# State space scan: ScalarE scales the turned u, TensorE turns it back, twelve states of sixteen

## The chip, the cores and the metric

The kernel runs on one core of one Trainium2 chip. The time is the device time of one execution in microseconds (us), as the median of several runs. Before the change it is 4166.02 us (three runs, 4165.89 to 4167.23).

## What is computed

The reference is a chain of four blocks over x of 8 sequences x 1024 tokens x 256 features. The change touches the first of them, a selective state space model with 16 states for each of 256 channels:

```
dt = softplus(x @ W_dt + b_dt);  A = -exp(A_log);  Bm = h @ W_B;  Cm = h @ W_C
decay = exp(dt[..., None] * A)                    # (T, B, D, N)
inp = (dt * x)[..., None] * Bm[:, :, None, :]     # (T, B, D, N), N = 16
s = decay * s + inp                               # over t, in order
y = einsum('bdn,bn->bd', s, c)                    # c = Cm at t
y = y + D_skip * x
```

Below, u = dt * x. For each state n, sequence b and half h of the channels (128 on the partitions), the input of the scan is u times the row B[n, :] over the 1024 tokens.

## The kernel before, in words

The program is a list of phases, one after the other: `ssm_inputs`, `ssm_scan`, `ssm_output`, then the delta, attention and expert phases. Only `ssm_scan` is touched. It goes through 8 batches (the sequences), each with 16 states n and 2 halves h, in this order; `own = n * H + h` (H = 2) numbers the 32 scans of a batch, `at` numbers them over all batches: 256 scans. Batches 1 to 6 run in a loop of three rounds with two batches each, the first and the last stand outside it.

For one scan:
- ScalarE makes the decay, exp(dt * A), 128 x 1024 elements (L606), into one of four buffers; it waits until the scan four before is done.
- The input, u times B's row, is put into PSUM, into `psI[h]`. There is one such tile for each half, so the input of scan k + 2 can only be made when scan k is done. For the states of `DIAG` (even n) TensorE does it: u was turned once for a batch, in chunks of 128 tokens (L632, copied by ScalarE to `uT`, L584), ScalarE fills `diag` with the identity times B's column of that chunk (L592, 8 instructions for a state, in two parts after each of the two exponentials of the state before, two buffers), and TensorE multiplies the turned u with it (L645, 8 chunks). For the states of `MIXED` (odd n) VectorE multiplies u by B's row, which a DMA has spread over the partitions (L703, right behind the scan before).
- VectorE scans (L724): `tensor_tensor_scan` over the 1024 tokens, decay and `psI[h]` in, one of four `state` buffers out.
- GpSimd multiplies the state by C's row (L575), into one of eight buffers `prod`.
- TensorE adds this to y in PSUM by a product with the identity (L656, two of 512 columns), three scans later (`LAG`). In its queue the step `own` holds the turn of the next u where it is due, then the input for scan `own + 1`, then the accumulation of scan `own - 3`.
- When the 16 states of a half are through, VectorE adds D_skip * x to y (L710, after scans 2 and 3 of the next batch), and the accumulation of the next batch's first state in that half waits for it.

Each engine has its own queue and works in order. They wait for one another by counting semaphores (`state_ready`, `inp_ready`, `dec_ready`, `prod_ready`, `y_added`, `uT_ready`, `diag_ready`). The turn of the next batch's u goes through `psI` too, at own = `TURN - 1` and `TURN`, where the states are mixed and TensorE doesn't need `psI`; `TURN` = `MIXED[3] * H` = 14. VectorE's L703 of that state waits until ScalarE has copied the turned u out (L701, L702). SyncE issues the loads; rows of B (512 KB, L520) are loaded for the mixed states alone.

Of the kernel before, what the change touches and what calls it, by code (L numbers as in the profile page):

```python
# [448 lines left out]
def ssm_scan(nc, A):  # L449
    CHUNKS = T // P  # L450
    ROWS = 4
    MIXED = tuple(range(1, S, 2))
# [3 lines left out]
    with ExitStack() as ctx:  # L456
# [6 lines left out]
        uT = [[m.sb(f"uT{k}{h}", [P, CHUNKS, P]) for h in two] for k in two]  # L463
        diag = [m.sb(f"diag{k}", [P, CHUNKS, P]) for k in two]
# [11 lines left out]
        diag_ready, dec_ready, inp_ready, state_ready = m.sem("diag"), m.sem("dec"), m.sem("inp"), m.sem("state")  # L476
# [4 lines left out]
        TURN = MIXED[3] * H  # L481
# [16 lines left out]
        with nc.Block() as block:  # L498
# [82 lines left out]
            def _(act):  # L581
                def turned(b, k, h):
                    act.wait_ge(u_turned, b * H + (h + 1))
                    act.activation(uT[k][h][:], psI[1 - h][:] if isinstance(b, int) and b == 0 else psI[h][:],  # L584
                                   ACT.Copy).then_inc(uT_ready, 1)

                def fill(b, n, part):

                    if part == 0 and (not isinstance(b, int) or b > 0 or DIAG.index(n) >= 2):
                        act.wait_ge(inp_ready, diag_count(b, n, 1) - 2 * H)  # L590
                    for c in range(4 * part, 4 * part + 4):
                        act.activation(diag[DIAG.index(n) % 2][:, c, :], ident[:], ACT.Copy,  # L592
                                       scale=b_col[:, bass.ds(b * CHUNKS + c, 1), n]).then_inc(diag_ready, 1)

                def batch(b, k, place):
                    for n in range(S):
                        for h in two:
# [9 lines left out]
                            if n in DIAG:  # L607
                                then = n + 1 if n + 1 in DIAG else n + 2
                                if then < S:
                                    fill(b, then, h)  # L610
                                elif place < 3:
                                    fill(b + 1, then - S, h)
# [9 lines left out]
                for h in two:  # L622
                    fill(0, 0, h)
                turned(0, 0, 1)
                act.wait_ge(a_made, 1)
# [3 lines left out]
            def _(pe):  # L629
# [5 lines left out]
                def scan_input(b, k, own, place):  # L635
# [3 lines left out]
                    pe.wait_ge(diag_ready, (b * ND + (order + 1)) * CHUNKS)  # L639
# [4 lines left out]
                    for c in range(CHUNKS):  # L644
                        last = pe.matmul(psI[h][:, c, :], uT[k][h][:, c, :], diag[order % 2][:, c, :], start=True, stop=True)  # L645
# [13 lines left out]
                def batch(b, k, place):  # L659
                    for own in range(PER):  # L660
# [9 lines left out]
                        elif H < own + 1 < PER and (own + 1) // H in DIAG:  # L670
# [2462 lines left out]
```

## Time and profile before

| | us |
|---|---|
| median of three runs | 4166.02 |
| profiled execution, its own time | 4168.11 |
| span of its instructions | 4166.5 |
| TensorE / VectorE / ScalarE / GpSimd busy | 3502 / 3254 / 2306 / 1370 |
| first scan starts, last starts | 272.2, 1070.8 |

The shares of busy time over the whole span mix eight phases with different limits. The scan is the stretch from some 250 to some 1080 us. One line of a view by line stands for all instructions of that line and shape: count, busy time (the union of their times), mean duration of one in ns, and the idle time of the engine just before them with what ended it. fp32 matmuls are recorded twice for each call, as they go through the array twice; a transpose is recorded once.

### The profile page before, as it was taken

What the parts mean: (1) busy time and instruction counts of PE and PEld (TensorE: products, weight loads), DVE (VectorE), ACT (ScalarE), POOL (GpSimd) and SP (SyncE); (2) the same over time, 40 slices, a digit from 0 to 9 for tenths busy, and PEclk for the clock granted to TensorE, in tenths of its full rate; (3) what the DMA queues carried; (4) which work ended last, traced back from release to release, by engine and by line L of the source; (5) the groups of instructions that cost most, each with busy time, mean ns of one, the idle gap of its engine ahead of it and who ended that gap; (6) DMA issues with size and microseconds to landing.
All of it is one profiled execution on the core that took longest, in us unless ns stands there. A gap on an engine that the chain in (4) does not pass through costs nothing. (4 is left out here: it accounts for less than half of the span.)

```text
span 4166.5 us, 65564 instructions
## 1 busy us (share of the span) xinstructions
PE 3502.2 (84%) x20079; PEld 2104.2 (51%) x20080; DVE 3253.8 (78%) x4239; ACT 2306.2 (55%) x4128; POOL 1369.6 (33%) x905
## 2 busy tenths in 40 slices
PE   8969888888657979989799999999999965379950
PEld 3445555555346868878233333333333324279950
DVE  8959999999786645657889898989899823368868
ACT  6755555555594533311288888888888851033323
POOL 4448888889302445410000000000000004645530
PEclk9989999999888989999599999999999985589975
DMA  6665444454677943377123232322222114222348
GB/s 218 248 207 175 164 163 162 162 172 137 206 253 189 253 119 106 91 195 221 40 52 74 52 73 52 71 55 64 61 59 66 30 42 133 89 77 90 92 159 293
DMA packets 536067, 538.10 MB, mean 129 GB/s; under 512 B 85296, under 2 KB 441776, under 8 KB 535648
## 3 DMA queue, kind: packets, MB, share of 16 engines
q1 hardware_dynamic: 521856, 497.23, 40.8%
q0 software_dynamic: 13952, 37.74, 2.6%
q8 instruction: 123, 2.02, 0.2%
q14 instruction: 136, 1.11, 0.1%
HBM read 317.93 MB, written 215.71 MB: 128 GB/s over the span
## 5 line engine op out<-in xcount | busy, mean ns | idle before, releaser
L2321 DVE TENSOR_REDUCE at_top<-at_psM 128x1 f32<-128x1024 f32 x1024 | 1206.1, 1220 | 136.5 <-PE at_psM L2172 135.4
L2281 ACT ACTIVATE at_probs<-at_psS 128x512 f32<-128x512 f32 x2048 | 1060.9, 603 | 250.8 <-PE at_psS L2198 250.8
L2198 PE MATMUL at_psS<-at_q,at_k 64*128 64x512 f32 x2048 | 795.3, 468 | 8.3 <-ACT at_probs L2281 8.3
L575 POOL TENSOR_TENSOR sc_prod<-sc_state,sc_c_row 128x1024 f32<-128x1024 f32 x256 | 709.1, 2789 | 117.2 <-DVE sc_state L724 109.0
L2172 PE MATMUL at_psM<-at_k,at_q 62*128 62x512 f32 x2048 | 689.7, 451 | 36.5 <-DMA at_vraw<-scratch_vf 21.9
L724 DVE TENSOR_TENSOR_SCAN sc_state<-sc_dec,sc_psI 128x1024 f32<-128x1024 f32 x256 | 578.4, 2280 | 53.3 <-PE sc_psI L645 29.5
L2172 PEld LDWEIGHTS at_psM<-at_k,at_q 62*128 62x128 f32 x2048 | 313.1, 190 | 601.8 <-DVE at_top L2321 519.8
L2211 PE MATMUL at_psV<-at_probs,at_v 128*32 128x512 f32 x4096 | 546.3, 605 | 0.0
L656 PE MATMUL sc_psY<-sc_prod,sc_ident 128*128 128x512 f32 x1024 | 467.4, 597 | 3.5 <-DVE sc_y L710 2.2
L606 ACT ACTIVATE sc_dec<-sc_dt,sc_a_exp 128x1024 f32<-128x1024 f32 x256 | 293.6, 1148 | 311.1 <-DVE sc_state L724 308.3
L2198 PEld LDWEIGHTS at_psS<-at_q,at_k 64*128 64x128 f32 x2048 | 337.6, 184 | 195.5 <-ACT at_probs L2281 190.6
L2139 POOL COPY at_v<-at_vraw 128x256 f32<-128x256 f32 x32 | 12.9, 403 | 1253.1 <-DMA at_vraw<-scratch_vf 1169.4
L645 PE MATMUL sc_psI<-sc_diag,sc_uT 128*128 128x128 f32 x2048 | 266.9, 285 | 91.8 <-DVE sc_state L724 86.9
L645 PEld LDWEIGHTS sc_psI<-sc_diag,sc_uT 128*128 128x128 f32 x2048 | 245.6, 196 | 184.2 <-DVE sc_state L724 136.8
L656 PEld LDWEIGHTS sc_psY<-sc_prod,sc_ident 128*128 128x128 f32 x1024 | 185.6, 193 | 185.2 <-issue 173.1
L2765 POOL DMA_INDIRECT scratch_ys<-ex_y,ex_slot x156 | 172.0, 1103 | 185.1 <-DVE ex_y L2898 138.9
L2352 PEld LDWEIGHTS ex_psY<-ek_w,ex_hid 128*128 128x128 f32 x1872 | 223.8, 188 | 3.9 <-issue 1.0
L2352 PE MATMUL ex_psY<-ek_w,ex_hid 128*128 x1872 | 224.9, 279 | 0.6 <-DVE ex_hid L2891 0.6
L703 DVE TENSOR_TENSOR sc_psI<-sc_u,sc_b_row 128x1024 f32<-128x1024 f32 x128 | 171.1, 1337 | 8.7 <-ACT sc_uT L584 8.7
L2491 POOL DMA_INDIRECT scratch_xs<-er_rows,ek_spot x128 | 129.5, 1012 | 115.9 <-DVE ek_spot L2652 72.6
L592 ACT ACTIVATE sc_diag<-sc_ident,sc_b_col 128x128 f32<-128x128 f32 x512 | 161.7, 387 | 6.3 <-PE sc_psI L645 6.3
L2785 ACT ACTIVATE ex_xT<-ex_psT 128x512 fp32r<-128x512 f32 x39 | 23.4, 600 | 253.4 <-PE ex_psT L2815 253.4
(393 smaller groups left out, 4941.4 us busy)
## 6 DMA issues: line engine op xcount, KB each, us to landing
sc_c_row<-scratch_bc SPq DMA_DIRECT2D x128, 512.0 KB, 4.3
scratch_xs<-at_zeros SPq DMA_DIRECT2D x140, 264.0 KB, 4.7
sc_b_row<-scratch_bc SPq DMA_DIRECT2D x64, 512.0 KB, 5.1
ec_y<-scratch_ys SPq DMA_DIRECT2D x32, 512.0 KB, 6.4
ex_x<-scratch_xs SPq DMA_DIRECT2D x39, 264.0 KB, 3.1
si_x<-in_x SPq DMA_DIRECT2D x16, 512.0 KB, 4.4
scratch_xn<-si_xn SPq DMA_DIRECT2D x16, 512.0 KB, 5.1
scratch_x_t<-si_xT SPq DMA_DIRECT2D x16, 512.0 KB, 5.7
```

The costliest lines, as they stand in the source:

```text
L575: pool.tensor_tensor(prod[:, (n * H + h) % 8, :], state[slot][:], c_row[n % ROWS][:], ALU.mult).then_inc(prod_ready, 1)
L606: act.activation(dec[slot][:], dt[k][h][:], ACT.Exp, scale=a_exp[:, h, n:n + 1]).then_inc(dec_ready, 1)
L645: last = pe.matmul(psI[h][:, c, :], uT[k][h][:, c, :], diag[order % 2][:, c, :], start=True, stop=True)
L656: last = pe.matmul(psY[h][:, cols], ident[:], prod[:, own % 8, cols], start=(n == 0), stop=(n == S - 1))
L724: dve.tensor_tensor_scan(state[slot][:], dec[slot][:], psI[h][:].rearrange("p c t -> p (c t)"), 0.0, ALU.mult, ALU.add).then_inc(state_rea ...
L2172: ins = pe.matmul(psM[t % 2][:, half * TILE:(half + 1) * TILE], rows_of(q4[j], h, 0, MAXROW)[:, c * P:(c + 1) * P], rows_of(k4[j], h, 0, M ...
L2198: pe.matmul(psS[v % 3][:], rows_of(k4[j], h, 0, GROUP)[:, c * P:(c + 1) * P], rows_of(q4[j], h, 0, GROUP)[:, half * TILE:(half + 1) * TILE ...
L2211: last = pe.matmul(psV[32 * h:32 * h + 32, :], v4[j][:, c, h, :], probs[:, slot(j, at_slot[4 * g + n]), :], start=(c == 0), stop=(c == KC ...
L2281: act.activation(probs[:, slot(j, v), :], psS[v % 3][:], ACT.Exp).then_inc(act_done, 1)
L2321: dve.tensor_reduce(top[j % 2][:, h, c:c + 1], psM[t % 2][:], AX.X, ALU.max, negate=True).then_inc(maxed, 1)
L2352: last = pe.matmul(out, a, b, start=start and n == 0, stop=stop and n == len(parts) - 1)
L2765: pool.indirect_dma_start(out=A["ys"], out_offset=bass.IndirectOffsetOnAxis(ap=slot[par][:, s:s + 1], axis=0), in_=y[par][:, s, :], in_off ...
```

## The change

Four states stay with VectorE (2, 6, 10, 14); the other twelve get their input from TensorE, in another way. ScalarE no longer scales the identity by B's column. It scales the turned u itself, both halves in one instruction: `scaled` is 128 tokens x 8 chunks x (2 x 128 channels), and each of the 8 instructions for a state is 256 elements wide instead of 128. TensorE then turns each chunk back (a transpose with the identity) into `psI[h]`. So `uT` becomes one tile for both halves, the first fill of a batch waits until both halves of u are turned, and `TURN` becomes `MIXED[2] * H` = 20.

```diff
-    MIXED = tuple(range(1, S, 2))
+    MIXED = (2, 6, 10, 14)
...
-        uT = [[m.sb(f"uT{k}{h}", [P, CHUNKS, P]) for h in two] for k in two]
-        diag = [m.sb(f"diag{k}", [P, CHUNKS, P]) for k in two]
+        uT = [m.sb(f"uT{k}", [P, CHUNKS, H, P]) for k in two]
+        scaled = [m.sb(f"scaled{k}", [P, CHUNKS, H, P]) for k in two]
...
-        TURN = MIXED[3] * H
+        TURN = MIXED[2] * H
...
-                    act.activation(uT[k][h][:], psI[1 - h][:] if isinstance(b, int) and b == 0 else psI[h][:],
+                    act.activation(uT[k][:, :, h, :], psI[1 - h][:] if isinstance(b, int) and b == 0 else psI[h][:],
...
-                def fill(b, n, part):
+                def fill(b, k, n, part):
 
                     if part == 0 and (not isinstance(b, int) or b > 0 or DIAG.index(n) >= 2):
                         act.wait_ge(inp_ready, diag_count(b, n, 1) - 2 * H)
+                    if DIAG.index(n) == 0:
+                        act.wait_ge(uT_ready, b * H + H)
                     for c in range(4 * part, 4 * part + 4):
-                        act.activation(diag[DIAG.index(n) % 2][:, c, :], ident[:], ACT.Copy,
-                                       scale=b_col[:, bass.ds(b * CHUNKS + c, 1), n]).then_inc(diag_ready, 1)
+                        act.activation(scaled[DIAG.index(n) % 2][:, c, :, :], uT[k][:, c, :, :], ACT.Copy,
+                                       scale=b_col[:, bass.ds(b * CHUNKS + c, 1), n]).then_inc(scaled_ready, 1)
...
                             if n in DIAG:
-                                then = n + 1 if n + 1 in DIAG else n + 2
-                                if then < S:
-                                    fill(b, then, h)
+                                order = DIAG.index(n) + 1
+                                if order < ND:
+                                    fill(b, k, DIAG[order], h)
                                 elif place < 3:
-                                    fill(b + 1, then - S, h)
+                                    fill(b + 1, 1 - k, DIAG[0], h)
...
-                for h in two:
-                    fill(0, 0, h)
                 turned(0, 0, 1)
+                for part in two:
+                    fill(0, 0, 0, part)
...
-                    pe.wait_ge(diag_ready, (b * ND + (order + 1)) * CHUNKS)
+                    pe.wait_ge(scaled_ready, (b * ND + (order + 1)) * CHUNKS)
...
-                        last = pe.matmul(psI[h][:, c, :], uT[k][h][:, c, :], diag[order % 2][:, c, :], start=True, stop=True)
+                        last = pe.transpose(psI[h][:, c, :], scaled[order % 2][:, c, h, :], ident[:])
...
-                        elif H < own + 1 < PER and (own + 1) // H in DIAG:
+                        elif H <= own + 1 < PER and (own + 1) // H in DIAG:
```

## Rows read from the trace of the kernel before

**Rows 1.** The page: busy time by engine, and one group of its section 5.

```profile
PE 3502.2 (84%) x20079; PEld 2104.2 (51%) x20080; DVE 3253.8 (78%) x4239; ACT 2306.2 (55%) x4128; POOL 1369.6 (33%) x905
...
L2281 ACT ACTIVATE at_probs<-at_psS 128x512 f32<-128x512 f32 x2048 | 1060.9, 603 | 250.8 <-PE at_psS L2198 250.8
```

**Rows 2.** By stretch: busy PE, PEld, DVE, ACT, POOL; clock, DMA share, GB/s.

```profile
474.00:576.00 102.00, 88.76 (x398) 54.02 (x397) 93.44 (x51) 56.63 (x98) 88.76 (x33) 0.98 0.50 172
```

**Rows 3.** By tile, sc_psI: count, duration ns min/median/max, first and last start us.

```profile
L724 DVE TENSOR_TENSOR_SCAN sc_state<-sc_dec,sc_psI x256: 2258/2286/2289, 272.2 to 1070.8; 128x1024 f32<-128x1024 f32 x128
```

**Rows 4.** By line, 272.2 to 1073.1 us: count, busy, mean, idle, releasers.

```profile
L575 POOL TENSOR_TENSOR sc_prod<-sc_state,sc_c_row 128x1024 f32<-128x1024 f32 x255 | 706.8, 2790 | 117.0 <-DVE sc_state L724 108.8 <-issue 7.9
L724 DVE TENSOR_TENSOR_SCAN sc_state<-sc_dec,sc_psI 128x1024 f32<-128x1024 f32 x256 | 578.4, 2280 | 53.3 <-PE sc_psI L645 29.5 <-DVE sc_psI L703 9.0 <-ACT sc_dec L606 8.3
...
L703 DVE TENSOR_TENSOR sc_psI<-sc_u,sc_b_row 128x1024 f32<-128x1024 f32 x128 | 171.1, 1337 | 8.7 <-ACT sc_uT L584 8.7
...
L710 DVE SCALAR_TENSOR_TENSOR sc_y<-sc_x,sc_skip,sc_psY 128x1024 f32<-128x1024 f32 x14 | 17.7, 1265 | 0.0
```

**Rows 5.** By tile, sc_prod: the same columns as rows 3.

```profile
L575 POOL TENSOR_TENSOR sc_prod<-sc_state,sc_c_row x256: 2347/2370/3356, 274.6 to 1073.1; 128x1024 f32<-128x1024 f32 x128
```

**Rows 6.** VectorE timeline, steady step: start us, length us, count, [idle before].

```profile
541.64 1.21 DVE L703 TENSOR_TENSOR sc_psI<-sc_u,sc_b_row 128x1024 f32<-128x1024 f32 x1
543.04 6.87 DVE L724 TENSOR_TENSOR_SCAN sc_state<-sc_dec,sc_psI 128x1024 f32<-128x1024 f32 x3 [0.19 <-ACT sc_dec L606]
549.83 1.35 DVE L703 TENSOR_TENSOR sc_psI<-sc_u,sc_b_row 128x1024 f32<-128x1024 f32 x1
...
553.57 1.21 DVE L703 TENSOR_TENSOR sc_psI<-sc_u,sc_b_row 128x1024 f32<-128x1024 f32 x1
```

**Rows 7.** Timeline, VectorE after the loop's jump back at some 571 us.

```profile
575.11 2.29 DVE L724 TENSOR_TENSOR_SCAN sc_state<-sc_dec,sc_psI 128x1024 f32<-128x1024 f32 x1 [3.75 <-PE sc_psI L645]
...
586.62 4.46 DVE L724 TENSOR_TENSOR_SCAN sc_state<-sc_dec,sc_psI 128x1024 f32<-128x1024 f32 x2
...
602.44 2.29 DVE L724 TENSOR_TENSOR_SCAN sc_state<-sc_dec,sc_psI 128x1024 f32<-128x1024 f32 x1 [1.68 <-PE sc_psI L645]
```

**Rows 8.** Timeline around a turn of u: scan input, accumulation, transposes, VectorE's L703.

```profile
507.28 2.05 PE L645 MATMUL sc_psI<-sc_diag,sc_uT 128*128 128x128 f32 x16
...
509.17 1.88 PE L656 MATMUL sc_psY<-sc_prod,sc_ident 128*128 128x512 f32 x4
...
510.46 0.14 PEld L632 LDWEIGHTS sc_psI<-sc_ident,sc_u 128*128 128x128 f32 x1 [0.24 <-issue]
510.88 1.04 PE L632 MATMUL sc_psI<-sc_ident,sc_u 128*128 128x128 f32 x8
...
511.76 1.88 PE L656 MATMUL sc_psY<-sc_prod,sc_ident 128*128 128x512 f32 x4
...
513.01 2.37 DVE L703 TENSOR_TENSOR sc_psI<-sc_u,sc_b_row 128x1024 f32<-128x1024 f32 x1 [1.21 <-ACT sc_uT L584]
```

**Rows 9.** Timeline of ScalarE: fills of the diagonal, exponentials back to back.

```profile
265.35 2.43 ACT L592 ACTIVATE sc_diag<-sc_ident,sc_b_col 128x128 f32<-128x128 f32 x8
...
273.00 3.22 ACT L606 ACTIVATE sc_dec<-sc_dt,sc_a_exp 128x1024 f32<-128x1024 f32 x3
```

**Rows 10.** Timeline of TensorE: transposes while the granted clock is 0.50.

```profile
262.42 3.67 PE L632 MATMUL sc_psI<-sc_ident,sc_u 128*128 128x128 f32 x16
```

**Rows 11.** Busy time by stretch at a batch's start: columns as in rows 2.

```profile
592.50:595.90 3.40, 1.15 (x8) 0.87 (x8) 3.21 (x3) 1.84 (x5) 2.96 (x2) 1.00 1.01 387
595.90:599.30 3.40, 3.40 (x13) 2.62 (x12) 3.21 (x3) 0.95 (x2) 3.05 (x2) 0.50 1.01 400
```

**Rows 12.** Delta stage by stretch: all, then L1591's transposes alone (PE, PEld, clock).

```profile
1722.30:1725.70 3.40, 2.09 (x17) 1.88 (x18) 1.82 (x8) 1.19 (x2) 2.45 (x2) 1.00 0.06 16
...
1722.30:1725.70 3.40, 1.28 (x8) 0.84 (x8) 1.00 0.06 16
```

More of the change, by code:

```diff
@@ L475, in ssm_scan @@
         b_turned, b_ready, u_turned, uT_ready = m.sem("b_turned"), m.sem("b_ready"), m.sem("u_turned"), m.sem("uT_ready")
-        diag_ready, dec_ready, inp_ready, state_ready = m.sem("diag"), m.sem("dec"), m.sem("inp"), m.sem("state")
+        scaled_ready, dec_ready, inp_ready, state_ready = m.sem("scaled"), m.sem("dec"), m.sem("inp"), m.sem("state")
         prod_ready, y_added, y_ready = m.sem("prod"), m.sem("y_added"), m.sem("y_ready")
```

## The prediction, made before the change was timed

> **What bounds the kernel now.** I read the page first [rows 1], and then only the state space scan, the one stage that the diff touches. It is bounded by four engines at once. One stretch of it shows VectorE busy 93 of 102 us, TensorE 89, GpSimd 89 and ScalarE 57, with the granted clock at 0.98 [rows 2], so what counts is how they hand work on. The scans (L724) start at 272.2 and the last ends at 1070.8 + 2.3 = 1073.1 us [rows 3]: 801 us of the run, and everything outside it stays as it is. In it VectorE has 256 scans, 128 products u·B (L703) and 14 outputs (L710): 578.4 + 171.1 + 17.7 = 767 us [rows 4], so VectorE sets the end. GpSimd's 707 us are inflated: a product costs 2.37 us in the median but 2.79 in the mean and up to 3.36 [rows 4, 5]. Taken one by one, those that overlap an L703 are the long ones.
>
> The steady step is read from VectorE's timeline [rows 6]. Two states (four scans: two mixed, two diagonal) take 553.57 - 541.64 = 11.93 us. The L703 at 541.64 holds the next scan back until 543.04, 1.40 us; the one at 549.83 holds the diagonal-to-mixed passage, and 549.83 to 553.57 is that L703 with its scan, 3.74 us. With 2.21 us for the scan this L703 costs 1.53, and the three scans between take 6.79, 2.26 each. 64 such steps make 764 us. The remaining 37 us are the 14 outputs (17.7), the seven turns of u (idle 8.7 in all), and some 11 us after idle ends at TensorE, among them 3.75 where the loop jumps back [rows 4, 7].
>
> **Part 1: VectorE.** Eight states were mixed, now four: 64 of the 128 L703 go. At (1.40 + 1.53)/2 = 1.46 each this is 94 us off VectorE. This is the most that the change can give.
>
> **Part 2: GpSimd.** It gets no new work and loses half of the overlaps. Before: 256 x 2.36 = 604 us if undisturbed, and 707 in fact, 103 more or 0.8 for each L703. Half of this goes, which leaves about 655 us. Per eight scans (the new pattern: one mixed state, three others): 8 x 2.36 + 2 x 0.8 = 20.5 us.
>
> **Part 3: TensorE.** The diagonal matmul goes through twice per chunk (16 records for 8 chunks); 507.28 to 509.17 is its hold on the engine, 1.89 us per scan input. The new transposes have the form of L632, which is one record per chunk. In the stream at full clock it holds the engine from 510.88 to 511.76, 0.88 us for eight [rows 8]. An accumulation into y (four records) holds it 510.88 - 509.17 = 1.71 us. Per eight scans TensorE had 4 x 1.89 + 8 x 1.71 = 21.2 us and gets 6 x 0.88 + 8 x 1.71 = 19.0. So the sum falls, but not where it hurts. In three neighbouring unmixed states each scan brings 0.88 + 1.71 = 2.6 us to TensorE and 2.26 to VectorE. I walked such a run of six scans: psI is single per half, so the input for scan k+2 can start only when scan k is over. Let the last mixed scan end at 0. The first input starts at 0.05 and takes 1.04 [rows 8] and 0.05 to be seen: ready at 1.14. The following start at 2.65, 5.25, 7.85, 10.45, each ready 1.1 later, at 11.55 the last. Scans want to start at 2.3, 4.5, 6.8, 9.1, 11.3. The first three inputs are in time, the fourth just, the fifth is 0.2 late. The run ends at 13.9 instead of 13.6 us. In the mixed state that follows, TensorE has 2 x 1.71 us of work in 7.4 us and catches up.
>
> So eight scans take 13.9 + 1.40 + 2.21 + 1.53 + 2.21 = 21.25 us, and 32 of them 680, against 764 before: **84 us less** (the 94 of part 1, less 10 that the runs give back).
>
> **Part 4: ScalarE.** L592 was 128 elements wide, 8 per state; it becomes 256 wide, 8 per state, and there are 12 states instead of 8. Its pace is 2.43/8 = 0.30 us, that of the exponentials (3.22 - 1.14)/2 = 1.04 us for 1024 elements [rows 9], which is 0.83 ns an element, so 0.30 + 0.11 = 0.41 us for 256. Bounds: 0.30 (width costs nothing), and 0.52, the pace of 512 wide (1060.9/2048) [rows 1]; I take 0.41. Per eight scans: 6 x (1.04 + 4 x 0.41) + 2 x 1.04 = 18.2 us, under 21.25. It is also early enough: the fill of a scaled buffer waits for the inputs of the state two before. In the run above the third state's fill can start at 1.14, and ends with the exponential between at 1.14 + 4 x 0.41 + 1.04 + 4 x 0.41 = 5.5; its input wants to start at 7.85. Nothing on the path, at 0.52 neither (6.3).
>
> **Part 5: what is moved.** The turn of the next u moves from state 7 to state 10, behind a full run. There TensorE is 1.7 us late instead of caught up, ScalarE then copies for 1.0 us, and VectorE's L703 waits for that: I get 1.35 us where the trace has 1.21 [rows 8], and over seven turns 1 us. The second copy of a turn now stands behind four wider fills on ScalarE (1.64 instead of 1.2 us) and is still in time. At the very start both copies and one fill of 8 x 0.41 precede the first input; but eight transposes replace sixteen passes at low clock (16 took 3.67 us there [rows 10]), so the first scan starts within 0.3 us of 272.2. Half of the 64 loads of B rows leave SyncE's queue; no transfer is waited for now, and no bound moves. The loop's jump back (3.75 us of idle, twice) stays.
>
> **Part 6: the clock.** At the batch's start, mixed state 2 stands behind two outputs on VectorE. TensorE cannot start y's accumulation for half 1 before the second output, and has no scan input to do meanwhile. I get 2.6 us of idle, then another 0.7 and 1.1. The trace shows what follows such a hole: TensorE busy 1.15 of 3.4 us, then clock 0.50 for the next 3.4 [rows 11], and then VectorE waits 1.68 us [rows 7]. This happened at two of seven batches before; I expect it at five or six, some at twice the length: 9 us more (bounds: 0, and 24 for seven twice 1.7).
>
> **Sum:** -84 + 1 + 9 + 1 (start, tail) = **-73 us**. The profiled execution (4168.1 us, 2.1 above the median of the runs) becomes 4095, the median **4093**.
>
> **A rule against it.** In the delta stage TensorE did transposes for 1.28 of 2.09 busy us in a stretch of 3.4, and the granted clock stayed at 1.00 [rows 12]. The Trainium skill (TensorE: Matmul & The Clock Gate, Part 4: PE-mode transpose) says the opposite: the full clock doesn't engage for transposes, they don't count as busy the same way. By that rule rival A below would be the case; by the row only the holes of part 6 count.
>
> **Rivals.**
> A. *The low clock wins (slower).* If transposes don't hold the clock up, TensorE falls to 1.2 GHz in the runs. Transposes took 3.67/16 = 0.23 us there [rows 10] against 0.11, so all of its work doubles: 38 us per eight scans, 1216 for the stage and the rest of 46: 460 us slower, about 4628. It decides from a share f of low clock at which 19.0 (1 + f) passes the 801/32 = 25.0 us of before: f = 0.32. For it: transposes are done in three of four states. The rule of the Trainium skill named above speaks for it as well. Against it: rows 12, and that accumulations stay 13.7 of every 19.0 us. Chance 0.06.
> B. *The hand-off is slower than my walk.* If a transpose batch that waited for its semaphore can't be prefetched, it holds TensorE for 0.42 us more (its first weights are loaded at 510.46, its first pass is at 510.88 [rows 8]), the pace in a run is 3.0, and its last input is ready at 13.2: 1.6 us more per run, 51 in all, so a gain of 22 us: 4144. Or ScalarE's wide copies double with their width, to 0.6: 6 x (1.04 + 2.4) + 2.08 = 22.7 us per eight scans, 47 us more: 4140. Both have milder forms; I put 4111 to 4156 here. Chance 0.22.
> C. *Full gain.* Two scans with early input run at (4.46 - 2.29) = 2.17 us apart [rows 7], less than 2.26. If TensorE keeps up and the clock stays, the whole 94 us and a little more come: 4062 to 4076. Chance 0.10.
> D. *The change doesn't do what it says:* the transposes of the scaled copies go through twice like matmuls. TensorE then has 6 x 1.89 + 13.7 = 25.0 us per eight scans, as much as the stage has now, and the runs are bound by 3.6 us a scan: 20.4 a run (the first input has 1.2 us of slack) and 7.35 for the mixed state, 27.8 x 32 = 889: 125 more than 764, 4293. Rows 8 speak against it. Chance 0.02.
> Something that just cancels the gain: 0.02. The forecast itself, 4076 to 4111: 0.58.
>
> **How the numbers follow.** The time is that of the forecast. From 4062 to 4135 lie C, the forecast and over half of B, about 0.82. A measurement of this kernel tells about 0.2% from no change, 8 us: faster is forecast, B and C, 0.90; A and D are slower, 0.08; 0.02 the same.
>
> **What the profile after would show.** 64 L703; scan inputs as 1536 single records, 8 in 0.9 us; ScalarE's fills at about 0.41 us pace and its busy time near 600 us in the stage; GpSimd's products 2.5 to 2.6 us in the mean; eight scans in 21.3 us; VectorE's idle before L724 put down to the transposes, small in the first half of a run and growing in its second; low clock after batch starts alone. I am wrong if VectorE waits in every scan of a run (B), if the clock is low inside runs (A), or if the fills set when transposes start.

## The result, and the profile after

The kernel after takes 4067.23 us (median of four runs, 4065.67 to 4072.39), beside 4165.95 for the kernel before on the same chip (4164.12 to 4167.23). The ratio is 0.977, with a 95% interval of 0.9757 to 0.9784: **99 us faster**, where 73 were forecast. It is inside the range of 4062 to 4135, but below the band of 4076 to 4111 that stood for the forecast's own mechanism, and inside the band of rival C. So two questions are open: which mechanism it was, and where some 25 us more come from. The profiled execution after has a time of its own of 4072.39, a span of 4070.8, so the profiled pair differs by 95.7. The page's busy time by engine, beside rows 1:

```profile
PE 3424.0 (84%) x19567; PEld 2028.8 (50%) x19568; DVE 3169.5 (78%) x4175; ACT 2440.9 (60%) x4384; POOL 1304.4 (32%) x905
```

VectorE has lost 84 us of work, GpSimd 65 without losing an instruction, and ScalarE has gained 135.

By line, from the first scan to the last, to be read against rows 4 (count, busy us, mean ns, idle before with its releasers). VectorE's product is now L705, the scan L726, the output L712, ScalarE's fill L594, GpSimd's product still L575:

```profile
L575 POOL TENSOR_TENSOR sc_prod<-sc_state,sc_c_row 128x1024 f32<-128x1024 f32 x255 | 646.4, 2564 | 84.4 <-DVE sc_state L726 73.5 <-PE sc_psY L658 5.8 <-issue 5.0
L726 DVE TENSOR_TENSOR_SCAN sc_state<-sc_dec,sc_psI 128x1024 f32<-128x1024 f32 x256 | 574.2, 2276 | 43.5 <-PE sc_psI L647 32.9 <-DVE sc_psI L705 6.9 <-POOL sc_prod L575 1.5
...
L594 ACT ACTIVATE sc_scaled<-sc_uT,sc_b_col 128x256 f32<-128x256 f32 x758 | 321.1, 494 | 95.3 <-PE sc_psI L647 95.3
...
L705 DVE TENSOR_TENSOR sc_psI<-sc_u,sc_b_row 128x1024 f32<-128x1024 f32 x64 | 86.1, 1346 | 8.7 <-ACT sc_uT L584 8.7
```

By tile, `sc_psI`, beside rows 3 (count, duration ns min/median/max, first and last start):

```profile
L647 PE MATMUL sc_psI<-sc_ident,sc_scaled x1536: 272/273/448, 271.1 to 976.4; 128*128 128x128 f32 x192
L726 DVE TENSOR_TENSOR_SCAN sc_state<-sc_dec,sc_psI x256: 2260/2286/2289, 273.0 to 977.6; 128x1024 f32<-128x1024 f32 x128
```

The change does what it says: 64 L705 instead of 128, and 1536 single records of transposes (12 states x 2 halves x 8 chunks x 8 batches), so rival D is out. From the first scan's start to the last's it is 704.5 us, where rows 3 give 798.6: **94.0 us of the 95.7 are in this stage**. Below, "the stage" is always this stretch, since it can be compared between chips. The waits of L726 for TensorE are 32.9 us where they were 29.5 [rows 4].

VectorE's timeline shows the steady pattern of eight scans (start us, length us, count, [idle before]):

```profile
570.50 1.21 DVE L705 TENSOR_TENSOR sc_psI<-sc_u,sc_b_row 128x1024 f32<-128x1024 f32 x1
571.90 2.29 DVE L726 TENSOR_TENSOR_SCAN sc_state<-sc_dec,sc_psI 128x1024 f32<-128x1024 f32 x1 [0.19 <-DVE sc_psI L705]
574.11 1.21 DVE L705 TENSOR_TENSOR sc_psI<-sc_u,sc_b_row 128x1024 f32<-128x1024 f32 x1
575.50 11.10 DVE L726 TENSOR_TENSOR_SCAN sc_state<-sc_dec,sc_psI 128x1024 f32<-128x1024 f32 x5 [0.19 <-DVE sc_psI L705]
586.91 2.29 DVE L726 TENSOR_TENSOR_SCAN sc_state<-sc_dec,sc_psI 128x1024 f32<-128x1024 f32 x1 [0.30 <-PE sc_psI L647]
589.50 2.29 DVE L726 TENSOR_TENSOR_SCAN sc_state<-sc_dec,sc_psI 128x1024 f32<-128x1024 f32 x1 [0.31 <-PE sc_psI L647]
593.00 2.33 DVE L705 TENSOR_TENSOR sc_psI<-sc_u,sc_b_row 128x1024 f32<-128x1024 f32 x1 [1.21 <-ACT sc_uT L584]
```

One scan of the pair in the mixed state stands at 571.90, the other at 575.50, 3.6 apart. The scans behind it need no wait until, at the end of the run, two wait 0.30 for TensorE, and they stand 589.50 - 586.91 = 2.59 apart. That is the 0.88 + 1.71 of the prediction. The eight steps of this group are 3.60, 3.60, 2.20, 2.18, 2.18, 2.25, 2.59, 2.59: **21.19 us, where 21.25 were forecast**. The same stretch of the other batches of the loop takes 21.2 to 21.3. Against 23.86 before (twice 11.93), over 32 such groups, this is 83 to 85 us less.

The other 10 us show in the lengths of batches (start of the first scan to that of the next batch). Before, the seven are 97.3, 99.8, 99.8, 104.7, 99.8, 104.5 and 99.8; after, 86.1, 89.2, 89.3, 89.4, 89.3, 89.1 and 89.1. **The two long batches are gone**: the fourth and the sixth, behind which the loop jumps back. That is 4.9 + 4.7 = 9.6 us. The sum of 93 to 95 stands against 94.0 measured. Two things lie in these 9.6, as the steps between scans show. The first step behind the jump is 3.5 and 3.3 us longer than in the other batches, 6.8 together. Some 30 us on, the scan at 602.44 that waits 1.68 for TensorE [rows 7] stands behind a stretch at clock 0.50 [rows 11]; there, and at the same place of the sixth batch, the steps are 1.4 longer, 2.8 together. The other batches of before have neither. The jump itself is visible in TensorE's queue, in the time of the branch at the loop's end (L486). First before, then after; count, duration ns min/median/max, first and last start; the 82 and 83 are the last round, where nothing is jumped:

```profile
L486 PEldq COMPARE_BRANCH  x3: 82/5062/5113, 566.1 to 974.9; - x3
```
```profile
L486 PEldq COMPARE_BRANCH  x3: 83/215/221, 535.5 to 892.5; - x3
```

Behind the jump of after, where a batch starts at 537.5, there is no 3.75 us hole as in rows 7:

```profile
530.78 11.20 DVE L726 TENSOR_TENSOR_SCAN sc_state<-sc_dec,sc_psI 128x1024 f32<-128x1024 f32 x5 [0.19 <-DVE sc_psI L705]
542.59 2.29 DVE L726 TENSOR_TENSOR_SCAN sc_state<-sc_dec,sc_psI 128x1024 f32<-128x1024 f32 x1 [0.61 <-POOL sc_prod L575]
```

The batch's beginning shows what became of the low clock:

```profile
550.47 2.28 DVE L726 TENSOR_TENSOR_SCAN sc_state<-sc_dec,sc_psI 128x1024 f32<-128x1024 f32 x1
552.67 1.20 DVE L705 TENSOR_TENSOR sc_psI<-sc_u,sc_b_row 128x1024 f32<-128x1024 f32 x1
554.06 6.64 DVE L726 TENSOR_TENSOR_SCAN sc_state<-sc_dec,sc_psI 128x1024 f32<-128x1024 f32 x3 [0.19 <-ACT sc_dec L608]
```

By stretch (busy PE, PEld, DVE, ACT, POOL; clock, DMA share, GB/s), the first beside rows 2, the others beside rows 11:

```profile
474.00:576.00 102.00, 92.33 (x381) 52.30 (x380) 95.70 (x49) 86.26 (x151) 93.11 (x38) 0.98 0.51 180
548.40:551.80 3.40, 1.20 (x3) 0.68 (x4) 3.40 (x3) 2.94 (x6) 3.18 (x1) 0.99 0.00 0
551.80:555.20 3.40, 3.40 (x11) 2.22 (x10) 3.21 (x3) 1.15 (x1) 2.29 (x1) 0.50 0.46 165
```

The clock falls behind TensorE's hole as it did before (busy 1.20 of 3.4 us, then 0.50, the level of 1.2 GHz). It does so at three of the seven batches, at 551.8, 640.5 and 729.3, each time for 3.4 us. But the three scans from 554.06 stand 2.2 apart without a wait: low clock and mixed state coincide, and there TensorE has time to spare.

### The profile page after: what moved, and what is told of

It reads as the page before. It is cut to its first block and busy times, and to the rows that moved or that the text cites. A ratio compares the mean times of both kernels' runs of the same rounds, so it can differ in the third digit from the quotient of the medians.

```text
span 4070.8 us, 64939 instructions
## 1 busy us (share of the span) xinstructions
PE 3424.0 (84%) x19567; PEld 2028.8 (50%) x19568; DVE 3169.5 (78%) x4175; ACT 2440.9 (60%) x4384; POOL 1304.4 (32%) x905
## 3 DMA queue, kind: packets, MB, share of 16 engines
q8 instruction: 103, 1.69, 0.2%
## 5 line engine op out<-in xcount | busy, mean ns | idle before, releaser
L575 POOL TENSOR_TENSOR sc_prod<-sc_state,sc_c_row 128x1024 f32<-128x1024 f32 x256 | 648.7, 2564 | 84.4 <-DVE sc_state L726 73.5
L726 DVE TENSOR_TENSOR_SCAN sc_state<-sc_dec,sc_psI 128x1024 f32<-128x1024 f32 x256 | 574.2, 2276 | 43.5 <-PE sc_psI L647 32.9
L658 PE MATMUL sc_psY<-sc_prod,sc_ident 128*128 128x512 f32 x1024 | 479.2, 598 | 15.6 <-DVE sc_y L712 15.6
L594 ACT ACTIVATE sc_scaled<-sc_uT,sc_b_col 128x256 f32<-128x256 f32 x768 | 325.2, 494 | 95.4 <-PE sc_psI L647 95.3
L608 ACT ACTIVATE sc_dec<-sc_dt,sc_a_exp 128x1024 f32<-128x1024 f32 x256 | 285.2, 1135 | 7.7 <-DVE sc_state L726 7.7
L647 PEld LDWEIGHTS sc_psI<-sc_ident,sc_scaled 128*128 128x128 f32 x1536 | 178.7, 143 | 179.2 <-DVE sc_state L726 82.6
L647 PE MATMUL sc_psI<-sc_ident,sc_scaled 128*128 128x128 f32 x1536 | 205.9, 278 | 60.5 <-DVE sc_state L726 53.6
L2213 PEld LDWEIGHTS at_psV<-at_probs,at_v 128*32 128x32 f32 x4096 | 80.6, 108 | 128.1 <-ACT at_probs L2283 85.6
```

What stands on the lines that cost most here:

```text
L575: pool.tensor_tensor(prod[:, (n * H + h) % 8, :], state[slot][:], c_row[n % ROWS][:], ALU.mult).then_inc(prod_ready, 1)
L594: act.activation(scaled[DIAG.index(n) % 2][:, c, :, :], uT[k][:, c, :, :], ACT.Copy, scale=b_col[:, bass.ds(b * CHUNKS + c, 1), n]).then_i ...
L608: act.activation(dec[slot][:], dt[k][h][:], ACT.Exp, scale=a_exp[:, h, n:n + 1]).then_inc(dec_ready, 1)
L647: last = pe.transpose(psI[h][:, c, :], scaled[order % 2][:, c, h, :], ident[:])
L658: last = pe.matmul(psY[h][:, cols], ident[:], prod[:, own % 8, cols], start=(n == 0), stop=(n == S - 1))
L726: dve.tensor_tensor_scan(state[slot][:], dec[slot][:], psI[h][:].rearrange("p c t -> p (c t)"), 0.0, ALU.mult, ALU.add).then_inc(state_rea ...
```

## The experiments

The stage of each, in us, and its difference from that of its base (before 798.6, after 704.5); expectations are on record as quoted. Ratios are to the kernel before on the same chip. The kernels that leave work out say so in their expectation.

| kernel | made from | ratio | stage | against its base |
|---|---|---|---|---|
| e1_odd_transposed | before, new method alone | 0.9972 | 787.7 | -10.9 |
| e2_diag_four | before, four mixed states alone | 1.0123 | 851.1 | +52.5 |
| e9_pe_half | after, half of TensorE's additions | 0.9757 | 699.7 | -4.8 |
| e10_pool_half | after, half of GpSimd's products | 0.9755 | 696.0 | -8.5 |
| e11_both_half | after, both halved | 0.9701 | 676.6 | -27.9 |
| e4_fill_split | after, twice the fills | 0.9872 | 746.6 | +42.1 |
| e3_quarters | after, longer loop on TensorE | 0.9791 | 709.1 | +4.6 |
| e6_before_unrolled | before, no loop | 0.9963 | 783.0 | -15.6 |
| e7_after_unrolled | after, no loop | 0.9755 | 697.7 | -6.8 |
| e8_early | after, mixed states one earlier | 0.979 | 708.6 | +4.1 |
| e5_two_mixed | after, two mixed states | 0.9738 | 686.3 | -18.2 |
| e12_changed_again | after, unchanged | 0.9765 | 705.6 | +1.1 |

The last row says how far two profiles of one kernel are apart: 1 us in the stage. The 95% intervals of the ratios reach 0.001 to 0.0045 to either side. By them e1, e2, e4, e6 and e11 differ from their bases; for the others the difference is read from the stage of one profile each.

**The halves of the change: method and number.** The new method with the eight mixed states of before:

```diff
-    MIXED = (2, 6, 10, 14)
+    MIXED = tuple(range(1, S, 2))
-        TURN = MIXED[2] * H
+        TURN = MIXED[3] * H
```

> The changed kernel with the eight odd states left to VectorE as before, so only the way of making the other inputs differs (scaled copies turned back). Theory (inputs that arrive earlier, and a TensorE loop that is short enough not to be fetched again): of four scans one that took 2.38 us before takes 2.2, 64 x 0.18 = 12 us, and the two long steps at the loop's jump (4.8 us each) go, 10 us: the scan stage takes 779 us instead of 799 to 801, the kernel is 20 to 22 us faster than before. Rival (only the number of products on VectorE counts): 0, within 3 us of before.

Ratio 0.9972 (0.9961 to 0.9983). The stage is 10.9 us shorter, and all of it but about one is the two long batches (its branch takes 0.22 us). The batches are 99.8 long as before, though the last scan of each run now comes after 2.18 instead of 2.38 us. The trace shows what eats this (both engines, same columns):

```profile
544.77 7.97 POOL L575 TENSOR_TENSOR sc_prod<-sc_state,sc_c_row 128x1024 f32<-128x1024 f32 x3 [0.36 <-DVE sc_state L726]
...
548.97 1.58 DVE L705 TENSOR_TENSOR sc_psI<-sc_u,sc_b_row 128x1024 f32<-128x1024 f32 x1
550.74 2.29 DVE L726 TENSOR_TENSOR_SCAN sc_state<-sc_dec,sc_psI 128x1024 f32<-128x1024 f32 x1 [0.19 <-ACT sc_dec L608]
552.94 1.21 DVE L705 TENSOR_TENSOR sc_psI<-sc_u,sc_b_row 128x1024 f32<-128x1024 f32 x1
554.34 6.64 DVE L726 TENSOR_TENSOR_SCAN sc_state<-sc_dec,sc_psI 128x1024 f32<-128x1024 f32 x3 [0.19 <-ACT sc_dec L608]
...
556.70 7.97 POOL L575 TENSOR_TENSOR sc_prod<-sc_state,sc_c_row 128x1024 f32<-128x1024 f32 x3 [0.36 <-DVE sc_state L726]
```

The L705 comes 0.2 us earlier, and takes 1.58 instead of 1.35 [rows 6] (1.21 where no product of GpSimd runs at its start). It ends 1.1 us after GpSimd's second product of these three (547.09 to 549.45), and the third is stretched to 3.33. The same 1.1 us (1.09 to 1.10) is found in before and after at every VectorE product that begins well before the end of a running one of GpSimd: it waits until that one is through. So the steady step closes over GpSimd and VectorE alone. From 544.77 on, GpSimd's two products last until 549.45, L705 until 550.55, its scan starts at 550.74, the next L705 at 552.94 and the next scan at 554.34, and GpSimd takes up that scan's state at 556.70: 11.93 us, and TensorE isn't in it. Before has the same 11.93. Both expectations missed: neither -20 nor zero.

Then the number alone: the mixed states of after with the diagonal matmul of before.

```diff
-    MIXED = tuple(range(1, S, 2))
+    MIXED = (2, 6, 10, 14)
...
-                                then = n + 1 if n + 1 in DIAG else n + 2
+                                order = DIAG.index(n) + 1
```

> The kernel before with states 2, 6, 10, 14 left to VectorE and twelve by the diagonal matmul, so only the number of states differs. Theory (TensorE sets the pace in a run of three unmixed states, 1.89 + 1.71 = 3.6 us a scan): 27.8 us for eight scans, the stage about 125 us longer than before, with VectorE idle before most scans of a run. Rival (VectorE's own work sets the end, 64 products of 1.46 us go): 94 us less than before.

Ratio 1.0123 (1.0094 to 1.0153), 52.5 us **longer**. In a run each scan waits for TensorE:

```profile
512.26 2.29 DVE L724 TENSOR_TENSOR_SCAN sc_state<-sc_dec,sc_psI 128x1024 f32<-128x1024 f32 x1 [1.22 <-PE sc_psI L645]
515.76 2.29 DVE L724 TENSOR_TENSOR_SCAN sc_state<-sc_dec,sc_psI 128x1024 f32<-128x1024 f32 x1 [1.22 <-PE sc_psI L645]
```

3.50 us apart, as 1.89 + 1.71 = 3.6 says, but two of the six inputs are early enough, so that eight scans take 25.8 and not rival D's 27.8 us; I had given the run too little slack at its start. The stage grows by 52.5 where 125 were expected. Method alone -11, number alone +52, together -94: neither half is worth its part of the whole. The one makes TensorE fast enough for the other.

**What bounds a run now.** There are two candidates: TensorE's 2.6 per scan, and GpSimd's products, which take some 2.36 each where a scan takes 2.18. Half of TensorE's additions into y are left out, or half of GpSimd's products, or both:

```diff
-                    for half in range(T // TILE):
+                    for half in range(T // TILE if n in (0, S - 1) else 1):
```
```diff
-                            pool.tensor_tensor(prod[:, (n * H + h) % 8, :], state[slot][:],
-                                               c_row[n % ROWS][:], ALU.mult).then_inc(prod_ready, 1)
+                            w = T if n < 4 else TILE
+                            pool.tensor_tensor(prod[:, (n * H + h) % 8, 0:w], state[slot][:, 0:w],
+                                               c_row[n % ROWS][:, 0:w], ALU.mult).then_inc(prod_ready, 1)
```

> The changed kernel with half of the accumulations into y left out (states 1 to 14 add 512 columns only), so TensorE holds 0.86 us instead of 1.71 per scan there; y is therefore incomplete. Theory (GpSimd binds too: six products of 2.36 us, 14.2 us, stand beside a run of six scans, and an L705 can't finish while the product before it runs): 0, at most 5 us less in the stage (704.5 us from first to last scan start); scans in a run 2.2 us apart, the L705 after a run stretched by some 0.8 us. Rival (TensorE alone sets the pace in a run): the run ends 0.8 us sooner, 26 us less.

> The changed kernel with half of each product on GpSimd left out for states 4 to 15 (512 of 1024 columns; y is wrong there), about 1.2 us instead of 2.36. Theory (TensorE binds in the runs): scans 10, 11 and the like stay 2.6 us apart, nothing gained, 0 to 5 us. Rival (GpSimd's port or its pace sets the eight scans): up to 26 us less.

> Both omissions together (half of the accumulations, half of the products). Theory (two bounds lie within 0.3 us of each other, so only taking both away shows VectorE's own): all scans in a run 2.2 us apart, eight scans in 8 x 2.2 + 2 x 1.4 = 20.4 us, 20 to 28 us less than the changed kernel. Rival (VectorE's own work and its latencies set the end already): under 8 us less.

VectorE's timeline with TensorE's half left out:

```profile
572.36 15.35 DVE L726 TENSOR_TENSOR_SCAN sc_state<-sc_dec,sc_psI 128x1024 f32<-128x1024 f32 x7 [0.19 <-DVE sc_psI L705]
588.69 3.42 DVE L705 TENSOR_TENSOR sc_psI<-sc_u,sc_b_row 128x1024 f32<-128x1024 f32 x1 [0.98 <-ACT sc_uT L584]
```

and GpSimd's of the same stretch:

```profile
584.01 7.00 POOL L575 TENSOR_TENSOR sc_prod<-sc_state,sc_c_row 128x1024 f32<-128x1024 f32 x3
```

Seven scans in a row now run 2.18 apart, no one waits for TensorE, and yet the stage gains 4.8 us alone. GpSimd's products come end to end, and the L705 that starts at 588.69, just after one of them has begun, takes 3.42 us: it ends at 592.11, 1.1 after GpSimd's product ends at 591.02. Outside the turn it is the same: the step at the passage to the mixed state grows from 3.60 to 3.72 in after to 4.59, and eight scans take 3.60 + 2.20 + 5 x 2.18 + 4.59 = 21.29, as many as in after. With GpSimd's half left out instead:

```profile
571.12 11.10 DVE L727 TENSOR_TENSOR_SCAN sc_state<-sc_dec,sc_psI 128x1024 f32<-128x1024 f32 x5 [0.19 <-DVE sc_psI L706]
582.53 2.29 DVE L727 TENSOR_TENSOR_SCAN sc_state<-sc_dec,sc_psI 128x1024 f32<-128x1024 f32 x1 [0.30 <-PE sc_psI L648]
585.12 2.29 DVE L727 TENSOR_TENSOR_SCAN sc_state<-sc_dec,sc_psI 128x1024 f32<-128x1024 f32 x1 [0.31 <-PE sc_psI L648]
588.61 1.23 DVE L706 TENSOR_TENSOR sc_psI<-sc_u,sc_b_row 128x1024 f32<-128x1024 f32 x1 [1.21 <-ACT sc_uT L585]
```

The run is as in after, 2.59 at its end. The 8.5 us come mostly from the turn, where the product takes 1.23 instead of 2.33 us (seven times 1.1 = 7.7). With both left out:

```profile
563.11 15.36 DVE L727 TENSOR_TENSOR_SCAN sc_state<-sc_dec,sc_psI 128x1024 f32<-128x1024 f32 x7 [0.19 <-DVE sc_psI L706]
580.19 1.23 DVE L706 TENSOR_TENSOR sc_psI<-sc_u,sc_b_row 128x1024 f32<-128x1024 f32 x1 [1.73 <-ACT sc_uT L585]
```

Fast scans and fast products, and 27.9 us less: twice what the two give singly, 13.3. So **two bounds lie on top of one another**, and only taking off both frees the stage: eight scans take 20.3 us. Rival C's mechanism (TensorE keeps up) is what this last kernel has and after has not. (In the first and the third of these kernels TensorE is less busy and its clock is at 0.50 in part of the stage; its scans come 2.18 apart all the same.)

**ScalarE.** Each fill in two instructions of 128 elements, so that its wide copies cost what rival B feared:

```diff
-                        act.activation(scaled[DIAG.index(n) % 2][:, c, :, :], uT[k][:, c, :, :], ACT.Copy,
-                                       scale=b_col[:, bass.ds(b * CHUNKS + c, 1), n]).then_inc(scaled_ready, 1)
+                        for side in two:
+                            last = act.activation(scaled[DIAG.index(n) % 2][:, c, side, :], uT[k][:, c, side, :], ACT.Copy,
+                                                  scale=b_col[:, bass.ds(b * CHUNKS + c, 1), n])
+                        last.then_inc(scaled_ready, 1)
```

> The changed kernel with each of ScalarE's fills made as two instructions of 128 elements instead of one of 256: twice as many, 0.60 us for what took 0.42. Theory (rival B of the prediction: per eight scans ScalarE needs 6 x (1.04 + 2.4) + 2.08 = 22.7 us and becomes the bound instead of 22.1 us for eight scans with outputs): 20 to 47 us more, and VectorE's idle before L726 is put down to fills or exponentials. Rival (ScalarE waits 95 us for TensorE's inputs now and takes the extra into that): under 8 us more.

Its fills between 273 and 980 us:

```profile
L595 ACT ACTIVATE sc_scaled<-sc_uT,sc_b_col 128x128 f32<-128x128 f32 x1448 | 440.5, 387 | 19.2 <-PE sc_psI L649 18.9
```

42 us more in the stage: rival B's +47 was a fair price for fills at 0.6, but they don't take that. In after four fills take 1.69 us in all, so (1.69 - 0.49)/3 = 0.40 each, against 0.41 forecast, and ScalarE waits 95.3 us for TensorE. Here this shrinks to 19.2, ScalarE is busy 99.6 of the 102 us from 474 to 576, and so has become the bound.

**The loop's jump.** What a theory has to say: why does the branch take 5.1 us before and 0.2 after? Counting TensorE's records in the trace between the two jumps, there are 1695 in a round before, 1452 after, 1182 in e1 and 2220 in e2. So the jump may be dear only above some length. To test it, after gets a longer round on TensorE without other work: the additions into y of states 1 to 14 in four matmuls of 256 columns instead of two of 512, 1900 records.

```diff
-                    for half in range(T // TILE):
-                        cols = slice(half * TILE, (half + 1) * TILE)
+                    width = 256 if 0 < n < S - 1 else TILE
+                    for part in range(T // width):
+                        cols = slice(part * width, (part + 1) * width)
```

> The changed kernel with the accumulations of states 1 to 14 cut into four matmuls of 256 columns instead of two of 512: the same columns, but 448 more instructions on TensorE in one round of the loop (1454 become about 1902; the kernel before has 1728). Theory (a round of more than some 1700 is fetched again each time and the jump back then stalls TensorE): instruction packets of TensorE's queue come back in rounds two and three, and two batches take 4 to 5 us more than their neighbours: 8 to 10 us more than the changed kernel. Rival (the jump costs the same, and the shorter inputs only hide it): no batch is longer than its neighbours by over 1 us. A slower pace of the narrower matmuls would lengthen all batches alike and is read apart from this.

The branch in e3, and then in e2:

```profile
L486 PEldq COMPARE_BRANCH  x3: 83/3372/3707, 535.9 to 896.4; - x3
```
```profile
L486 PEldq COMPARE_BRANCH  x3: 83/5787/6262, 586.8 to 1023.0; - x3
```

The queues in rounds two and three (540 to 900 us; packets, MB, share; "instruction" is a fetch of code), in after and then in e3:

```profile
q1 hardware_dynamic: 16304, 59.38, 47.2%
q14 instruction: 21, 0.17, 0.2%
```
```profile
q1 hardware_dynamic: 16084, 58.55, 47.1%
q8 instruction: 19, 0.31, 0.3%
q14 instruction: 21, 0.17, 0.2%
```

In after, queue 8 has nothing to fetch there; in e3 it works again. In the kernel before it fetches in the loop as well, here within 360 to 570 us:

```profile
q8 instruction: 8, 0.13, 0.3%
```

So up to 1584 records a round (e5, below, whose branch takes 0.22) are kept, and from 1695 on they are fetched anew. That the number of records decides, and not where the code lies in memory, is tested by e3 alone. The Trainium skill (Runtime: NRT & Kernel Launch, Instruction fetch mechanics) gives TensorE 128 KiB for 2048 instructions, and says that a taken branch out of the current window forces a fetch of the target, an instruction fetch stall. The second half agrees with the branch of 3.4 to 6.3 us; the runs show besides that a shorter loop is spared the fetch, and that the number from which it isn't, counted in records, lies between 1584 and 1695 and so below 2048. The stage, though, grows by 4.6 us alone and not by 9.6: the two batches are 90.7 and 90.9 long, some 1.4 more than the others. After the jump VectorE waits 0.79 and 0.91 (rows 7 had 3.75):

```profile
540.97 2.29 DVE L727 TENSOR_TENSOR_SCAN sc_state<-sc_dec,sc_psI 128x1024 f32<-128x1024 f32 x1 [0.79 <-PE sc_psI L647]
544.17 2.29 DVE L727 TENSOR_TENSOR_SCAN sc_state<-sc_dec,sc_psI 128x1024 f32<-128x1024 f32 x1 [0.91 <-PE sc_psI L647]
```

The expectation of 8 to 10 is missed: the stall is shorter here than before, 3.4 to 3.7 instead of 5.1, and more of it lies beside other work. What is shown: the round's length decides on the stall, and the stall makes a batch longer. How much of the branch stays visible depends on what lies beside it: 3.5 and 3.3 of 5.1 before, 5.1 and 4.8 of 6.3 and 5.8 in e2, and 1.4 here. The other side is to take the loop away altogether:

```diff
-            batch(0, 0, 1)
-            with eng.Fori(0, (B - 2) // 2) as turn:
-                for k in two:
-                    batch(turn * 2 + (k + 1), 1 - k, 2)
-            batch(B - 1, 1, 3)
+            for b in range(B):
+                batch(b, b % 2, 1 if b == 0 else 3 if b == B - 1 else 2)
```

> The kernel before with the eight batches written out, no loop, all else the same. Theory (the two long batches, 104.7 and 104.5 us beside 99.8, are the loop's jump back and the low clock behind it): all inner batches take 99.8 us and the stage 10 us less. Rival (they come from the work at these places, such as the y stores or loads): the two batches stay 4.8 us longer.

> The changed kernel with its eight batches written out, no loop. Theory (with constants in the waits a mixed scan starts 0.15 us sooner, as it did in the kernel before without its loop, 3.45 instead of 3.60 us; there is no jump to save, since the loop isn't fetched again): 8 x 0.15 = 1.2 us for each of the six inner batches, 7 us less than the changed kernel in all. Rival (TensorE's and GpSimd's pace in the runs takes it back): 0 to 2 us.

In the kernel before this gives 15.6 us (ratio 0.9963, 0.9948 to 0.9979). The jump is gone, and in the steady step four scans take 11.62 instead of 11.93, so the first of the loop's six batches is 97.4 long instead of 99.8. The other five are 98.9: in each, and in the last batch of all, the clock is at 0.50 for 3.4 us behind the hole at the batch's start, and a scan input of TensorE comes due there. This is the scan behind the stretch from 489.2 to 492.6 us:

```profile
496.07 2.29 DVE L721 TENSOR_TENSOR_SCAN sc_state<-sc_dec,sc_psI 128x1024 f32<-128x1024 f32 x1 [1.40 <-PE sc_psI L642]
```

So the low clock costs 1.5 us a batch with the diagonal matmul, jump or no jump; over these six batches that is an estimated 9 us which e6 would have gained besides. The expectation (99.8 for all inner batches, 10 us less in all) missed this and the shorter step. In after it gives 6.8 us against the first profile and 7.9 against that of the same chip: no jump left to save, but the loop's batches are 87.7 to 87.9 instead of 89.2 (87.9 where the clock falls, 87.7 where it doesn't). Both have the same reason in the steps: in the mixed state a scan with its product takes 3.45 instead of 3.60. All engines' waits compare with constants there instead of register values. In e6 VectorE's pause between a product and its scan shrinks from 0.19 to 0.04 us, and GpSimd's before its three products from 0.35 to 0.20; how much each of them is worth wasn't tried. The times, 4065.95 (0.9732 to 0.9777 by ratio) and 4069.67 for after again (0.9741 to 0.9788), overlap, so the gain is seen in the trace alone.

> The changed kernel itself once more, on the chip of the three others, so that they can be compared with it there: 0.977 of the kernel before, the stage 704 to 706 us from first to last scan start.

**The place of the mixed states.** One state earlier, so that mixed state 1 fills TensorE's hole at the batch's start:

```diff
-    MIXED = (2, 6, 10, 14)
+    MIXED = (1, 5, 9, 13)
```

> The changed kernel with states 1, 5, 9, 13 left to VectorE instead of 2, 6, 10, 14: same work, but the run of three states follows directly on the two outputs at the batch's start. Theory (the hole of some 2 us on TensorE there lowers its clock, and now no mixed state lies behind it to take up the delay): at each batch start where the clock falls, scans of the run are 1.7 to 3 us late in all, 5 to 12 us more than the changed kernel. Rival (only the number of states and the length of the runs count): within 3 us.

The stage is 4.1 us longer than in after and 3.0 longer than in e12, between the two expectations, with two profiles of one kernel 1.1 apart. The clock falls at two batches alone (at 369.8 and 639.5), and the first of these stretches ends at 373.2, just as the run starts at 373.1, so what was to be tested hardly occurred. This run decides nothing.

**Further on the same way.** If a VectorE product costs more than a scan input of TensorE, two mixed states should be better still:

```diff
-    MIXED = (2, 6, 10, 14)
+    MIXED = (5, 12)
-        TURN = MIXED[2] * H
+        TURN = MIXED[1] * H
```

> The changed kernel with two states left to VectorE (5 and 12) instead of four, the next u turned at state 12. Theory (in a run the pace is TensorE's 2.6 us a scan, and each mixed state is also the pause in which TensorE and GpSimd catch up): runs of 16 and 12 scans take .05 + 2.6 (R - 2) + 1.1 + 2.3 = 39.9 and 29.5 us, two mixed states 14.7, together 84.1 us a batch where the same sum gives 84.8 for the changed kernel: 1 us less a batch, 5 us less in all, within 10 us of the changed kernel's 704.5. Rival (each product that VectorE is spared gives 1.46 us, as on the way from eight states to four): 32 x 1.46 = 47 us less.

```profile
575.55 2.29 DVE L726 TENSOR_TENSOR_SCAN sc_state<-sc_dec,sc_psI 128x1024 f32<-128x1024 f32 x1 [0.31 <-PE sc_psI L647]
578.14 2.29 DVE L726 TENSOR_TENSOR_SCAN sc_state<-sc_dec,sc_psI 128x1024 f32<-128x1024 f32 x1 [0.30 <-PE sc_psI L647]
```

18 us less in the stage and 4057.58 us, ratio 0.9738 (0.9709 to 0.9767): the fastest of the complete kernels, though its interval overlaps that of after. I had expected about -5. The steps of a batch say why it is more: four products less save 4 x 1.4 = 5.6 us, the steps at TensorE's pace of 2.59 instead of 2.18 rise from 7 to 13 and give 6 x 0.4 = 2.4 back, and the product behind the long run costs 0.4 more, as GpSimd's isn't through. That is 2.8 us a batch; the loop's batches are 86.7 long in the mean instead of 89.2, which is 2.5. VectorE's wait for TensorE rises to 47.7 us from 32.9, so this way is near its end.

## Why the prediction was right, and where not

- **What bounds the kernel, and parts 1 and 3 (-84 us).** Right in the size, 21.2 to 21.3 a group instead of 21.25, and in what ends a run: TensorE at 2.59 a scan, with the last scan of a run 11.8 us behind the first where the walk had 11.55. Two readings inside it were off without harm. Scans that wait for nothing come 2.18 apart and not 2.26, and so the last two or three of a run are late and not the last alone; since TensorE's pace sets the run's end, this changes nothing in the sum. It also means that 94 us is not the most that could be had. And in before VectorE doesn't set the pace alone: GpSimd's products are in the cycle of 11.93 (e1). e9 to e11 confirm that TensorE bounds the runs, together with GpSimd.
- **Part 2 (GpSimd).** The sum was right: 646 us against 655, 2.56 in the mean against 2.5 to 2.6. What I made of its 20.5 us per eight scans, that GpSimd is no bound, was the wrong step: I treated the overlap of L705 as a cost to GpSimd alone. The product of VectorE waits for GpSimd's running product too (1.21 becomes up to 2.33 in after and 3.42 in e9), so that GpSimd's phase enters VectorE's path. It cost nothing in the sum, since this bound lies where TensorE's does; but whoever had planned the next step from my account, say faster additions, would have got the 5 us of e9, not the 26 of its rival.
- **Part 4 (ScalarE).** Right: 0.40 a fill; busy 321 + 284 + 14 = 619 us in the stage against 600. e4 shows the price where it would be wrong.
- **Part 5 (turn, start).** The turn's wait was 1.21, not 1.35, and the step 6.01 where it was 6.05; the first scan starts 0.8 us later than before, but at the same 272.2 in e12. **The sentence that the loop's jump back stays is wrong by 6.8 us.** I knew the idle by its releaser only (rows 7: TensorE's scan input) and had not asked what TensorE did in that time. The branch of 5.1 us stood in its queue, and was a matter of the loop's length, which the change shortens by 243 of 1695 records.
- **Part 6 (clock, +9 us).** The hole came as walked (2.52 instead of 2.6 us) and the clock fell behind it, at three batches (two in e12) and not at five or six. The price of 1.7 us each was carried over from the kernel before, where a scan input from TensorE came due in the low stretch [rows 7]. Now a mixed state lies there, which I had in my own walk. A fall of the clock costs 0.1 to 0.2 us (e7, where batches with it are 87.9 and without it 87.7). So not only do the 9 us not come, the 2.8 that before lost in this way are gone too: this term, put at +9, is about -3.
- **The rule of the Trainium skill** (TensorE: Matmul & The Clock Gate, Part 4: PE-mode transpose) that the full clock doesn't engage for transposes isn't borne out here. The granted clock is 0.98 over 102 us in which transposes run in three states of four, and it falls only behind holes. Accumulations are still most of TensorE's work there (474 us busy beside 204), so this shows the clock of the mixture and not of transposes alone. Rival A is out.
- **Rivals.** The time lies in C's band, but not by C: the runs do wait for TensorE. The forecast's mechanism holds, with two terms mis-sized by 12 (clock) and 7 (jump), both towards the gain: -84 + 1 + 1 - 3 - 7 = -92, where 94 to 96 were measured. They moved the time 26 us below the forecast and out of its own band. That it is still inside the range is luck in part: it lies in a piece of the range that was there for rival C, whose mechanism didn't occur. The medians differ by 99, of which 3 are the spread of single executions (4065.67 to 4072.39).

## What to carry to other kernels

A stall has to be followed to what the engine named did in that time, its branches included; a releaser's name (the instruction that ended the wait) doesn't by itself say whether a change will move it. When two engines are near their limit, taking work off one tells little: halve each alone, and then both, before planning the next step. And moving work to an engine pays when its own instruction becomes cheaper first: here the number of states alone cost 52 us, and with the cheaper transpose it gained 94.

## What the runs showed of the hardware beyond what I expected

- A loop of 1452 or 1584 TensorE records a round jumps back in 0.22 us and isn't fetched again; loops of 1695, 1900 and 2220 took 5.1, 3.4 to 3.7, and 5.8 to 6.3 us a jump, with instruction queue 8 at work in the loop's rounds.
- A VectorE product of two SBUF operands, begun while GpSimd multiplies, ends 1.1 us after GpSimd's running product (1.58 in e1, 2.33 in after and 3.42 in e9, instead of 1.21), and GpSimd's next one takes 3.2 to 3.3 instead of 2.36. VectorE's scans of decay and PSUM aren't held in this way: they take 2.26 to 2.29 beside GpSimd's products.
- The pace of ScalarE is 0.30 us for a copy of 128 elements, 0.40 for one of 256, and 1.04 for the exponential of 1024 [rows 9, and four fills in 1.69 us after].
- A loop's waits cost more than those of the same code written out: four scans of before take 11.93 us in the loop and 11.62 without it (e6).
